# Last stage: half of the weighted projections go from VectorE alone to ScalarE and GpSimd

## The reference

```
n1 = layernorm(x, ln1_w, ln1_b)
rw = gating(n1)                                  # 8 weights for each token
q = einsum('btc,ech,bte->bth', n1, q_proj, rw)   # k and v in the same way
scores = einsum('bth,bsh->bts', q, k) * scale    # causal
attn = einsum('bts,bsh->bth', softmax(scores), v)
attn_out = einsum('bth,ehc,bte->btc', attn, o_proj, rw)
hs = x + attn_out
n2 = layernorm(hs, ln2_w, ln2_b)
rw2 = gating(n2)
inter = gelu(einsum('btc,eci->btei', n2, w1))
out = hs + einsum('btei,eic,bte->btc', inter, w2, rw2)
```

## Time and profile before

| what | value |
|---|---|
| median of 3 runs | 2651.24 us (2650.6 to 2653.67) |
| the profiled execution's own time | 2659.23 us |
| its span in the profile | 2657.4 us |
| busy share of PE, DVE, ACT, POOL | 81%, 82%, 64%, 54% |
| mean granted TensorE clock | 0.895 of full |

### The profile page before, as it was taken

How to read it: one execution, slowest core, us unless ns; L and a number is a source line. 1 busy time by engine, 2 the same in 40 slices (tenths; PEclk the granted TensorE clock), 3 DMA queues, 4 the chain that set the end, 5 groups by cost and what they waited for, 6 DMA issues and landing times.

```text
span 2657.4 us, 41448 instructions
## 1 busy us (share of the span) xinstructions
PE 2144.9 (81%) x14994; PEld 1428.2 (54%) x14994; DVE 2187.8 (82%) x3754; ACT 1698.9 (64%) x2686; POOL 1440.2 (54%) x1323
## 2 busy tenths in 40 slices
PE   3433897688599597999898989998987698779888
PEld 1101555356266375566566656666655447654675
DVE  6999789889978313999999999999999892679445
ACT  6443687687566444989898988998997214220422
POOL 0545334633634201777987798789878503580157
PEclk7555799799699798999999999999999799789989
DMA  2000000000000000111111111111110000000000
GB/s 117 0 0 0 1 1 1 1 1 2 19 1 1 1 13 20 29 27 36 25 25 25 25 25 25 25 25 25 25 49 1 24 1 1 1 16 1 1 1 17
DMA packets 22666, 42.17 MB, mean 16 GB/s; under 512 B 6592, under 2 KB 7104, under 8 KB 22080
## 3 DMA queue, kind: packets, MB, share of 16 engines
q1 hardware_dynamic: 22464, 39.52, 5.6%
HBM read 12.23 MB, written 2.10 MB: 5 GB/s over the span
## 4 chain that ended last, share of the span: by engine, by line
DVE 34%; PE 28%; issue 18%; POOL 10%; ACT 10%; DMA 0%; POOLq 0%; DVEq 0%; ACTq 0%; SPq 0%
DVE MA L1325 11%; PE ps L889 4%; DVE WB L1334 4%; PE ps L1156 2%; DVE BIG L338 2%; PE ps L1185 2%; PE ps L2048 2%; POOL MA L422 2%; ACT WB L1253 2%; ACT HR L790 2%; PE ps L1168 2%; DVE BIG L344 1%; PE ps L1983 1%; POOL WB L1409 1%; PE ps L818 1%
## 5 line engine op out<-in xcount | busy, mean ns | idle before, releaser
L1325 DVE TENSOR_REDUCE MA<-ps 128x1 f32<-128x1024 f32 x512 | 607.2, 1214 | 25.9 <-PE ps L1156 19.6
L422 POOL TENSOR_TENSOR MA<-MA,BIG 128x1024 f32<-128x1024 f32 x128 | 312.9, 2468 | 437.4 <-DVE BIG L344 437.4
L1253 ACT ACTIVATE WB<-ps,MA 128x1024 f32<-128x1024 f32 x397 | 444.4, 1126 | 55.1 <-DVE MA L1325 52.9
L1156 PE MATMUL ps<-BIG 96*128 96x512 f16 x1024 | 310.1, 384 | 75.4 <-ACT WB L1253 63.4
L889 PE MATMUL ps<-WB,HR 128*128 128x128 f32 x2304 | 287.7, 283 | 7.9 <-DVE acc L725 7.9
L889 PEld LDWEIGHTS ps<-WB,HR 128*128 128x128 f32 x2304 | 279.8, 198 | 24.3 <-issue 11.4
L790 ACT ACTIVATE HR<-ps,second 128x512 f32<-128x512 f32 x288 | 191.1, 688 | 129.1 <-PE ps L820 128.3
L1409 POOL TENSOR_SCALAR WB<-WB,MA 128x384 f32<-128x384 f32 x192 | 267.5, 1393 | 9.3
L1168 PE MATMUL ps<-first,WB 128*128 128x128 f32 x1640 | 225.4, 279 | 18.0 <-POOL WB L1412 17.1
L1790 POOL TENSOR_TENSOR BIG<-MA,BIG 128x512 f32<-128x512 f32 x64 | 66.0, 1050 | 265.5 <-DVE MA L1674 184.8
L1168 PEld LDWEIGHTS ps<-first,WB 128*128 128x128 f32 x1640 | 183.0, 142 | 41.9 <-POOL WB L1412 21.7
(11 more groups left out here) (315 smaller groups left out, 4973.2 us busy)
## 6 DMA issues: line engine op xcount, KB each, us to landing
BIG<-BIG SPq DMA_DIRECT2D x192, 64.0 KB, 2.0
BIG<-MA SPq DMA_DIRECT2D x192, 64.0 KB, 2.0
WB<-w_dram SPq DMA_DIRECT2D x1, 2304.0 KB, 14.5
X<-x_dram SPq DMA_DIRECT2D x4, 512.0 KB, 15.7
HR<-w_dram SPq DMA_DIRECT2D x1, 2048.0 KB, 9.5
out_dram<-X SPq DMA_DIRECT2D x8, 256.0 KB, 2.0
BIG<-wqkv_dram SPq DMA_DIRECT2D x1, 1536.0 KB, 6.3
WB<-w_dram SPq DMA_DIRECT2D x2, 512.0 KB, 5.1
```

The costliest lines, as they stand in the source:

```text
L422: e.tensor_tensor(yy[:, c, :], yy[:, c, :], db[n % 2][c], ALU.add).then_inc(*p_my.up(b, n, c))
L1156: x = e.matmul(ps[s][:, 512 * h:512 * h + 512], stack[q % 2][0:96, 0, 2 * pp + s, 128 * i:128 * i + 128], stack[q % 2][0:96, 1, 2 * pp + s ...
L1253: e.activation(P_of(n, s), ps[s][:, :], ACT.Exp, bias=L[:, 2 * s + pp:2 * s + pp + 1], scale=1.0, accum_out=L[:, 4 + 2 * s + pp:5 + 2 * s ...
L1325: e.tensor_reduce(L_of(n)[:, c:c + 1], ps[s][:, :], AX, ALU.max, negate=True).then_inc(*v_amx.up(n, s))
```

## The change

DVE keeps the products of the even experts (x = 0, 2, 4, 6), the list `EVEN`. Those of the odd experts, the list `ODD`, are read from PSUM by ACT, which multiplies with the weight and writes 128x384 into one of two buffers in SBUF (`odd_rows`, buffer n % 2), and POOL adds the buffer to `s_acc` (`odd_pool`). DVE's addition for an even expert now waits for POOL's of the odd expert before it, and POOL's for DVE's. PE waits before product n for ACT where product n - 4 is an odd one. All transposes of q and k wait for POOL's last addition (n = 63). The table `D_AT` has new numbers for almost every step of the stage.

```diff
-        D_AT = {'period': 197.51, 'shift': 0.21,
...
-'pr': 9.6, 'prK': -0.05, 'acc': -14.88, 'qt': -7.25, 'qe': 6.09,
...
+        D_AT = {'period': 198.4, 'shift': 0.23,
...
+'pr': 13.06, 'prK': -0.03, 'acc': -20.53, 'asc': -0.64, 'padd': -4.77, 'qt': 20.95, 'qe': 18.76,
...
+        EVEN, ODD = ([(n,) for n in range(64) if n // 2 % 2 == i] for i in range(2))
...
-        v_dlo, v_dac = two("v_dlo", *keys(2)), two("v_dac", *keys(64))
+        v_dlo, v_dac = two("v_dlo", *keys(2)), two("v_dac", *EVEN)
+        a_dsx, p_dac = two("a_dsx", *ODD), two("p_dac", *ODD)
...
-                for n in range(64):
+                for n, in EVEN:
...
-                        e.wait_ge(*v_dac[k].at(r, n - 2))
+                        e.wait_ge(*p_dac[k].at(r, n - 2))
...
+        def odd_rows(k, n):
+            return s_sc[k][n % 2][:, 0:384].rearrange("p (a c) -> p a c", a=3)
+
+        def odd_pool(e, k):
+            for r in range(2):
+                for n, in ODD:
+                    j, x = tile_expert(n)
+                    yield d_proj(k, r, n, "padd")
+                    e.wait_ge(*a_dsx[k].at(r, n))
+                    e.wait_ge(*v_dac[k].at(r, n - 2))
+                    to = s_acc[k][:, :, j, :]
+                    e.tensor_tensor(to, to, odd_rows(k, n), ALU.add).then_inc(*p_dac[k].up(r, n))
...
+                for n, in ODD:
+                    j, x = tile_expert(n)
+                    yield d_proj(k, r, n, "asc")
+                    e.wait_ge(*t_dpr[k].at(r, n))
+                    if n == 2:
+                        e.wait_ge(*v_dgt[k].at(r, 0, "rw"))
+                    if n >= 6:
+                        e.wait_ge(*p_dac[k].at(r, n - 4))
+                    elif r:
+                        e.wait_ge(*p_dm[k].at(r - 1, 12 + n))
+                    e.activation(odd_rows(k, n), B[n % 4][:, 0:384].rearrange("p (a c) -> p a c", a=3), ACT.Copy,
+                                 scale=G(6)[:, j, x:x + 1]).then_inc(*a_dsx[k].up(r, n))
...
-                        e.wait_ge(*v_dac[k].at(r, n - 4))
+                        e.wait_ge(*(a_dsx if n // 2 % 2 else v_dac)[k].at(r, n - 4))
...
-                        e.wait_ge(*v_dac[k].at(r, 63 if a + h else 60))
+                        e.wait_ge(*p_dac[k].at(r, 63))
```

More of the change, by code:

```diff
@@ new lines, in program @@
+        D_AT = {'period': 198.4, 'shift': 0.23, 'sims': 1.38, 'simsA': 2.84, 'simsP': 4.02, 'simsV': 13.66, 'w0': 13.86, 'w1': -53.58, 'wK': -21.82, 'stats0': -0.28, 'norm0': 2.07, 'stats1': 3.73, 'norm1': 8.99, 'gain': -7.39, 'bias': 5.78, 'turn0': 16.63, 'square0': 14.72, 'sum0': 5.85, 'logits0': 17.08, 'pick0': 1.13, 'exp0': 27.97, 'weights0': 67.52, 'root0': 17.7, 'scale': 18.47, 'scaleh': 15.95, 'scaleK': -1.36, 'hi': 1.5, 'lo': 0.28, 'pr': 13.06, 'prK': -0.03, 'acc': -20.53, 'asc': -0.64, 'padd': -4.77, 'qt': 20.95, 'qe': 18.76, 'q': 17.7, 'k': -7.98, 'v': 6.51, 'evict': 12.47, 'att0': 71.13, 'att1': 82.46, 'att2': 88.15, 'att3': 95.14, 'att4': 98.33, 'att5': 100.47, 'att6': 109.68, 'att7': 123.22, 'att8': 117.94, 'inverse': 2.14, 'turnP': 1.77, 'evictP': 1.83, 'out': 2.85, 'o': 120.56, 'oK': -7.14, 'oscale': -19.72, 'oturn': -16.4, 'oevict': 8.35, 'omul': 11.07, 'oadd': 8.03, 'stats2': 117.2, 'norm2': 132.37, 'turn2': 154.49, 'square2': 129.1, 'sum2': 154.37, 'logits2': 162.92, 'pick2': 119.68, 'exp2': 171.84, 'weights2': 165.47, 'root2': 142.19, 'up': 162.83, 'upK': 1.3, 'gelu': 7.79, 'down': 19.73, 'weigh': 4.5, 'add': 4.12, 'end_stats': 14.36, 'end_norm': 16.22, 'end_x': 16.14, 'n_stats0': 148.15, 'n_norm0': 164.29, 'n_stats1': 167.82, 'n_norm1': 171.22, 'n_gain': 10.91, 'n_bias': 2.45, 'n_square0': 184.49, 'n_sum0': 188.32, 'n_root0': 189.21, 'n_K': 1.35}
@@ L2135, in _ @@
                   opening_pool(e))
-            weave(attention(attend_pool, e, "pool"), experts_pool(e), open_pool(e, 0), open_pool(e, 1), soft_pool(e, 0), soft_pool(e, 1), end_pool(e, 0), end_pool(e, 1))
+            weave(attention(attend_pool, e, "pool"), experts_pool(e), open_pool(e, 0), open_pool(e, 1), odd_pool(e, 0), odd_pool(e, 1), soft_pool(e, 0), soft_pool(e, 1), end_pool(e, 0), end_pool(e, 1))
         @block.sync
```

1 line of the change is left out of this document (removed).

## The result

The changed kernel takes **2668.2 us** (median of 5 runs, 2668.1 to 2673.6); the kernel before took 2651.6 beside it (5 runs, 2650.6 to 2659.2). The ratio is 1.0062, 95% interval 1.0049 to 1.0076: slower by some 16.6 us, where I had predicted 2653.8 us, at most 2668.

The account below looks back on a forecast made before the run. DVE was taken to bound the projections, by only 0.036 us a product over PE. The terms +7.2 - 1.1 - 2.1 - 1.0 - 2.2 + 1.8 = +2.6 us on 2651.24 gave 2653.8 us, range 2641 to 2668.

Parts of the forecast that it names:

- the opening: Start of the last stage: a few swaps on DVE and POOL, costed at nothing, covered by DVE's full list.
- Rival (d): Swaps in the opening, or sums before round 1, cost more: 2656 to 2660 us; chance 0.10.
- Rival (e): Projections: PE's gaps grow from 7% to 13%, its clock halves for part of them: over 2668 us; chance 0.04.
- The loop: Projections: a ring of waits through POOL, DVE, PE and ACT, 4.5 us for eight products, 0.56 us each against 0.525.
- (b): Projections: shorter ring, POOL's addition nearer 0.84 us or ACT's copy at 0.49: 2642 to 2645 us; chance 0.20.
- (c): Projections: POOL's addition slower, 1.1 to 1.3 us: 2657 to 2671 us; chance 0.24.
- The gap between the sequences closes: Projections: sequence 0's transposes now stand behind while PE, ACT and POOL run on: -2.26 us a round.
- Start of round 1: Two sums of 1.22 us now on DVE between last statistics and gating, half of `split_dve` moved behind: +1.8 us.
- Output projection, second norm: Behind attention: -0.55 us a round for fewer waits on POOL, -1.06 for statistics falling in sequence 1's units.
- Early gelus: Experts: sequence 0's first two gelus before sequence 1's exponential: -1.0 us in round 0, -2.2 in round 1.
- let through: Experts, round 0: POOL busy 23.00 of the last 23 us, so half of the gain was counted: -1.0 us.
- The time before: Base of the forecast: median of plain runs 2651.24 us, 8.0 below the profiled execution of 2659.23.

Follow-up runs that it names:

- apart: The change, with the odd experts' sum in a place of its own, so VectorE waits for GpSimd no more: 2655.9 us, ratio 1.0006 against the kernel before.
- short_add: The change, with GpSimd's addition on queries and keys alone, 256 of 384 columns (odd values left out): 2654.1 us, ratio 0.9998 against the kernel before.
- weights_in: The change, with the four operations making sequence 1's weights moved to the middle of sequence 0's additions: 2673.2 us, ratio 1.0073 against the kernel before.
- again: Unchanged kernels run for second profiles: the kernel before 2652.5 us (ratio 0.9996), the change 2669.7 us (1.0056).
- order_only: The kernel before with the new table of due times, VectorE still weighting and adding all experts: 2656.4 us, ratio 1.0007 against the kernel before.
- split_only: The changed program with the old table of due times and the two new keys: 2669.3 us, ratio 1.0056 against the kernel before.

## Why the prediction was wrong

**The step that failed is the opening**: "a few swaps on DVE and POOL that I cost at nothing; what covers them is DVE's own full list there". I looked at the two engines that I took for busy. The swap that cost 7 of the 7.8 us was on TensorE, which had waits there to spare, and just these were what the moved units had filled; without them its clock stayed at half until 2104.2 and not 2086.9. Rival (d) had the place, but a power on POOL as mechanism and 3 us as price. Rival (e) had the mechanism, the clock, but put it into the projections, where the clock stayed at full (1.00 in the window above).

**The loop** was right: no engine full, VectorE half busy, 0.571 us a product (0.56), the prices 0.581 and 0.997 us (0.58 and 1.00), hence (b) and (c) both wrong. `apart` and `short_add` show it from two sides. Sequence 1 with its tail, to the first scores, costs +3.4 us in either round (38.6 for 35.1), predicted 3.9.

**"The gap between the sequences closes (-2.26 us)"** failed: the loop itself runs +1.6 us from first to first read-out where I had -0.4. I counted the transposes that lay in the gap and not VectorE's four operations (1.4 us) that lay in it with them. (The 2.26 us are also a reading too high: 2.72 us between the starts less a step of 0.525 are 2.20.) Of the 2 us a round that this term was off, `weights_in` shows 1.2 to 1.4 as these operations, but only 0.6 to 0.9 of it to be had back, as sequence 1 then takes longer.

**Start of round 1**: +2.8 us behind the last addition, predicted +1.8. The sums are 1.7 of it, the moved transposes 0.6.

**Output projection, second norm**: -1.4 us in round 0 and, with the clock alike, -1.4 to -1.6 in round 1, where -1.6 was predicted: right. The -3.0 of the first profile was in part luck with the clock.

**Early gelus**: they win 2.7 us in round 0 and 1.3 to 3.4 in round 1 (predicted 1.0 and 2.2), but the additions of round 0 end where they did before (85.8 us behind the norm's gain, 85.9 before), so the 1.0 us that I "let through" was none. GpSimd's list shows where it went. From its first addition there to its last it waits 3.5 us for 5.2, but it starts 0.7 us later, and its work takes 0.9 us longer. Four of its additions last 2.25 us in place of 1.27. They lie beside VectorE's gain and bias of round 1's norm (lines 1760 and 1764); before, two additions and one operation of line 1820 were as slow, beside the same work of VectorE. GpSimd and VectorE in the change:

```profile
2359.56 13.80 POOL L1809 TENSOR_TENSOR MA<-MA,BIG 128x512 f32<-128x512 f32 x8
...
2361.94 2.17 DVE L1764 TENSOR_TENSOR MA<-MA,lnp 128x1024 f32<-128x1024 f32 x1
```

From round 1's last gain to the end the change wins 0.8 us against before, predicted 2.2, with the clock at half for 23.9 us in both profiles; its second profile, with less time at half, has 2.9. No run takes back the other orders of that stretch one by one, so what they cost there stays open.

**The time before** was itself uncertain. With the prediction's 2651.2 from three runs I took the profiled 2659.2 as the odd one; in 29 runs beside `again`, `order_only`, `split_only` and `apart` the kernel before had a median of 2657.3 (2647.7 to 2660.1), beside the others 2653.3 to 2653.5. The differences between kernels are read from profiles that start the stage alike, or from lengths within it.

## What to carry to other kernels

When a new order moves work on an engine that waits, ask what its waits held. Here small units of another stage had filled TensorE's waits; with them gone its clock rose 17 us later, on an engine that no one had as the bound. When work is split over three engines, cost the loop of waits and not the load of each; an own target for each writer, added together later by an engine that is not waited for, opens the loop at no more work. And before two profiles are compared, look at a mark that stands ahead of the change, and at where the granted clock was down in each.

## What the runs showed of the hardware that I had not expected

Added work made the last stage's opening shorter: with 32 transposes more on TensorE it took 76.7 us for 82.0 and 81.6, with the clock at full for the logits (1.85 us for the first 16 small matmuls and not 3.42). GpSimd's addition of 128x512 takes 1.27 us beside VectorE's operations that read PSUM and SBUF (line 1716), and 2.25 us beside VectorE's that read both inputs from SBUF (lines 1760, 1764). ScalarE's copy from PSUM with a scale read from a column is 0.581 us for 384 columns, the plain one 0.492. Some stretches repeat from profile to profile to 0.1 us and less (16.88 and 16.89 us before, 19.67 and 19.67 in the change, from the last addition of round 0 to round 1's first read-out). Others come at levels 1.5 to 2.1 us apart in one and the same program, by where the clock is down (103.05 and 104.66 us, 85.1 and 83.0 in the change), while whole executions differ by up to 12 (2647.7 to 2660.1).
